# GpSimd's order in an attention loop turned round: normalisation of a unit ahead of the moments of the next one

## The chip, the cores and the metric

The kernel runs on one core of a Trainium2 chip. The metric is the time of one execution on the device in microseconds. Three runs are given by their median. One more execution was recorded by the hardware profiler, and all that is read from a trace comes from it.

## The reference

`x` and `ctx` are (128, 64, 128) in float32: 128 sequences of 64 rows with 128 features. Two layers follow each other.

```
x = x + xattn0(layernorm(x), ctx, ctx)     # layer norms on q and kv, 16 heads of 8, sigmoid gate, layer norm on the output
x = x + ffn0(layernorm(x))                 # silu(w1 x) * (w2 x), two 512x512 with gelu, back to 128
x = x + xattn1(layernorm(x), ctx, ctx)     # 16 heads of 8, no gate, no norm of ctx
x = x + ffn1(layernorm(x))                 # relu(x W1 + b1) W2 + b2
```

`layernorm` takes mean and variance of each row. The attention is a full softmax over the 64 rows of the same sequence.

## The kernel before

`x` lies in SBUF for the whole run as 64 tiles of 128 rows. The kernel is a row of stages: preparation of the weights, attention of layer 0, its feed-forward part, attention of layer 1, its feed-forward part. Each stage is a block in which the five engines have an instruction list of their own, and only semaphores order one engine against another.

`attention(nc, t, layer, front)` is one function for both layers; `gated` is true in layer 0. It works on units of two tiles (256 rows, four sequences), so N = 32 units. On every engine a function `step(j)` is unrolled for j = −5 to N + 3, and one step holds work of several units in different phases. The order within a step is written by hand, and each engine takes its list strictly in order (a later instruction doesn't overtake one that waits).

A unit i goes through these phases:

- VectorE takes the statistics of x, in layer 0 of ctx too (L827), and aggregates them to mean and variance (L842, gives `moments_ready`) in step i − 5.
- GpSimd makes from them minus the mean (L709), the variance with epsilon added (L712, L713 or L715), the power −0.5 of it (L717, `rstd`) and their product (L721, `offset`, gives `offset_ready`), also in step i − 5. The power and the product wait on a chain semaphore for the operation before.
- GpSimd normalises the tiles in step i − 4 (L730, `normed`, gives `normed_ready`): four 128x128 operations in layer 0 (two tiles of x, two of ctx), two in layer 1. `normed` has two slots, so this waits for `in_t_done` of the unit two before.
- TensorE transposes `normed` into the PSUM bank `ps_turn` (L556, gives `in_t_done`) in step i − 3, ScalarE takes it to SBUF (L643, `turned`).
- In step i − 2 TensorE makes the gate (L574, layer 0 only), values (L608), queries and keys (L613, L614); ScalarE takes them; SyncE copies queries and keys into a block layout with DMAs (L904).
- In step i TensorE makes the scores (L513 ahead of all else in the step), VectorE takes the maximum of each row (L765, `top`), TensorE transposes it (L580), and VectorE and ScalarE split it in two parts (L649, L795), which SyncE lays out by DMA (L893).
- In step i + 1 TensorE starts PSUM with the negated maximum (L588), adds the scores again in the other orientation (L513), and ScalarE takes the exponential (L660).
- In step i + 2 TensorE multiplies with the values (L541), ScalarE takes the result (L634, `av`), TensorE turns it (L597), VectorE divides by the sums (L810, L812, `heads_out`).
- In step i + 3: L529, L629 and the output projection (L564), its bias and statistics on VectorE (L784, L834, L848, L853), the power for the output's norm on GpSimd (L737, `y_scale`). In step i + 4 VectorE scales it and adds it to x (L774, `y_gain`, and L802). In layer 1 it is only the sum (L788).
- GpSimd adds the closing bias to the rows of x (L742) in step i.

TensorE's order in a step j, shortened to the lines above: scores of j (L513), L529, L541, L556 of j + 3, L564, L574, L580, L588 and L513 of j − 1, L597, L608, L613, L614. L580 and L588 wait for both halves of L765. The next step's scores wait for the exponentials of ScalarE. SyncE's order: L893 of j, the load of ctx for j + 8 (in layer 0 it waits for `normed_ready` of unit j + 4, whose slot it takes), L904 of j + 2.

Of the kernel before, what the change touches and what calls it, by code (L numbers as in the profile page):

```python
# [11 lines left out]
ALU = mybir.AluOpType  # L12
# [6 lines left out]
P = 128  # L19
# [7 lines left out]
UNROLL = 4  # L27
UNIT_TILES = 2
# [5 lines left out]
def wait(eng, sem, count):  # L34

    if isinstance(count, int) and count <= 0:
        return
    eng.wait_ge(sem, count)


def span(i, width):

    return slice(i * width, (i + 1) * width) if isinstance(i, int) else bass.ds(i * width, width)
# [82 lines left out]
def front_power(nc, t, front, pool, i, s):  # L126

    wait(pool, front.spread_ready, i + 1)
    wait(pool, front.norm_ready, i + 1 - front.slots)
    nc.gpsimd.tensor_tensor(front.rstd[:, s, :], front.spread[:, s, :], t.minus_half[:, 0:CHUNK_TILES],  # L130
                            ALU.pow).then_inc(front.rstd_ready, 1)
# [251 lines left out]
def attention(nc, t, layer, front):  # L383
# [10 lines left out]
    NORMS = 2 if gated else 1  # L394
    SEQS = UNIT_TILES * PER_TILE

    def on(i):
        return 0 <= i < N
# [9 lines left out]
    with ExitStack() as ctx:  # L408
        def sb(name, shape, dt=F32):
            return ctx.enter_context(nc.sbuf_tensor(f"{name}{layer}", shape, dt))  # L410
# [4 lines left out]
        def sem(name):  # L415
            return ctx.enter_context(nc.semaphore(f"{name}{layer}"))
# [4 lines left out]
        rstd = sb("rstd", [P, UNROLL, NORMS, UNIT_TILES])  # L421
        minus_mean = sb("minus_mean", [P, UNROLL, NORMS, UNIT_TILES])
        offset = sb("offset", [P, UNROLL, NORMS, UNIT_TILES])
        normed = sb("normed", [P, 2, NORMS, UNIT_TILES, P])
# [13 lines left out]
        ctx_in = sb("ctx_in", [P, UNROLL, UNIT_TILES, P])  # L438
# [21 lines left out]
        offset_ready = sem("offset_ready")  # L460
        normed_ready = sem("normed_ready")
        in_t_done = sem("in_t_done")
# [39 lines left out]
        with nc.Block() as block:  # L502
# [193 lines left out]
            @block.gpsimd  # L696
            def _(pool):
                for s in range(UNROLL):
                    nc.gpsimd.memset(qk_sets[:, s, :, :, :], 0.0).then_inc(zeros_ready, 1)
                nc.gpsimd.tensor_copy(shift[:, :, :].rearrange("p s n -> p (s n)"),  # L700
                                      t.zero[:, 0:1].to_broadcast([P, 1024])).then_inc(zeros_ready, 1)

                def step(j):
                    i = j + 5
                    if on(i):
                        s = i % UNROLL
                        wait(pool, moments_ready, i + 1)
                        wait(pool, normed_ready, i - 3)
                        nc.gpsimd.tensor_scalar(minus_mean[:, s, :, :], moments[:, s, :, :, 0], -1.0, 0.0, ALU.mult, ALU.add)  # L709
                        if gated:  # L710

                            nc.gpsimd.tensor_scalar(spread[:, s, 0, :], moments[:, s, 0, :, 1], 1.0 + EPS, EPS * EPS, ALU.mult, ALU.add)  # L712
                            nc.gpsimd.tensor_scalar(spread[:, s, 1, :], moments[:, s, 1, :, 1], 1.0, EPS, ALU.mult, ALU.add).then_inc(pool_chain, 1)  # L713
                        else:
                            nc.gpsimd.tensor_scalar(spread[:, s, 0, :], moments[:, s, 0, :, 1], 1.0, EPS, ALU.mult, ALU.add).then_inc(pool_chain, 1)  # L715
                        wait(pool, pool_chain, 2 * i + 1)
                        nc.gpsimd.tensor_tensor(rstd[:, s, :, :], spread[:, s, :, :],  # L717
                                                t.minus_half[:, 0:NORMS * UNIT_TILES].rearrange("p (n k) -> p n k", n=NORMS),
                                                ALU.pow).then_inc(pool_chain, 1)
                        wait(pool, pool_chain, 2 * i + 2)  # L720
                        nc.gpsimd.tensor_tensor(offset[:, s, :, :], minus_mean[:, s, :, :], rstd[:, s, :, :], ALU.mult).then_inc(offset_ready, 1)  # L721
                    i = j + 4
                    if on(i):
                        s = i % UNROLL
                        wait(pool, offset_ready, i + 1)
                        wait(pool, in_t_done, i - 1)
                        for n in range(NORMS):
                            for k in range(UNIT_TILES):
                                src = ctx_in[:, s, k, :] if n else t.x[:, span(i * UNIT_TILES + k, P)]
                                last = nc.gpsimd.tensor_scalar(normed[:, i % 2, n, k, :], src, rstd[:, s, n, k:k + 1],  # L730
                                                               offset[:, s, n, k:k + 1], ALU.mult, ALU.add)
                        last.then_inc(normed_ready, 1)
                    i = j - 3
                    if gated and on(i):
                        wait(pool, y_spread_ready, i + 1)
                        wait(pool, x_done, i - 3)
                        nc.gpsimd.tensor_tensor(y_scale[:, i % UNROLL, :], y_spread[:, i % 2, :], t.minus_half[:, 0:UNIT_TILES],  # L737
                                                ALU.pow).then_inc(y_scale_ready, 1)
                    if on(j):
                        wait(pool, normed_ready, j + 1)  # L740
                        rows = t.x[:, span(j, UNIT)].rearrange("p (k d) -> p k d", d=P)
                        nc.gpsimd.tensor_tensor(rows, rows, closing_row.unsqueeze(1).to_broadcast([P, UNIT_TILES, P]), ALU.add).then_inc(biased, 1)  # L742
                    if j == N:
                        front_power(nc, t, front, pool, 0, 0)

                for j in range(-5, N + 4):
                    step(j)
# [663 lines left out]
```

## Time and profile before

| | |
|---|---|
| median of three runs | 1193.12 us (1189.18 to 1199.44) |
| the profiled execution | 1191.88 us, of which the span from first to last instruction is 1190.0 us |
| mean granted clock of TensorE over the span | 0.938 of full speed |
| TensorE matmuls busy | 1010.8 us (85%) |
| VectorE / ScalarE busy | 711.1 us (60%) / 745.3 us (63%) |
| GpSimd busy | 310.1 us (26%) |
| attention of layer 0, its loop with scores | about 59 to 400 us |
| attention of layer 1 | about 780 to 1070 us |

Times in the trace count from the first instruction. "PE" is TensorE's matmuls and "PEld" its weight loads, DVE is VectorE, ACT ScalarE, POOL GpSimd, SPq SyncE's queue of DMA issues. A number in brackets behind a row is the idle time of that engine just before it and who ended it; "issue" means that nothing in the trace ended it. A granted clock of 1.00 is 2.4 GHz and 0.50 is 1.2 GHz; a window with a value between holds both.

### The profile page before, as it was taken

How to read it: one execution, taken by the hardware profiler on the slowest of the kernel's cores; microseconds unless marked ns; L12 is line 12 of the kernel's file. 1: busy time of each engine (PE TensorE's matmuls, PEld its weight loads, DVE VectorE, ACT ScalarE, POOL GpSimd, SP SyncE). 2: the span in 40 equal slices, each digit the busy share in tenths (PEclk: the TensorE clock that was granted, in tenths of full speed). 3: DMA queues.
4: the chain of work that ended last, by engine and by line, in shares of the span. 5: the costliest groups of instructions: out<-in, count | busy, mean ns of one | idle time of the engine just before them, and what ended most of it. 6: DMA issues, size and time to landing. Idle time of an engine off the chain costs nothing. (4 is left out here: it accounts for less than half of the span.)

```text
span 1190.0 us, 42024 instructions
## 1 busy us (share of the span) xinstructions
PE 1010.8 (85%) x16955; PEld 785.3 (66%) x16955; DVE 711.1 (60%) x1894; ACT 745.3 (63%) x1347; POOL 310.1 (26%) x655
## 2 busy tenths in 40 slices
PE   3378878877888579999999999848899898988998
PEld 2356666666666368788788887636666676666886
DVE  4256566566656666666766766324555555448995
ACT  3145455455545568888888888515556565656896
POOL 5644444344441100000000000053233333301110
PEclk8599898899989789999999999958999999998999
DMA  8311111111101000000000000011111111100111
GB/s 246 86 48 40 46 43 35 46 45 40 44 28 34 4 1 1 0 0 0 0 0 0 0 0 1 1 41 54 55 58 52 59 52 56 44 24 5 41 44 54
DMA packets 53367, 42.43 MB, mean 36 GB/s; under 512 B 16784, under 2 KB 42128, under 8 KB 53200
## 3 DMA queue, kind: packets, MB, share of 16 engines
q1 hardware_dynamic: 50976, 39.61, 10.7%
q8 instruction: 127, 2.08, 0.8%
q0 software_dynamic: 352, 0.27, 0.2%
q10 hardware_dynamic: 1872, 0.14, 0.1%
q14 instruction: 40, 0.33, 0.1%
HBM read 16.93 MB, written 4.19 MB: 18 GB/s over the span
## 5 line engine op out<-in xcount | busy, mean ns | idle before, releaser
L765 DVE TENSOR_REDUCE top<-ps_w 128x16 f32<-128x1024 f32 x128 | 150.8, 1219 | 113.9 <-PE ps_w L513 113.9
L915 PE MATMUL g_ps<-g_h_lo,w_hi 128*128 128x512 f32 x512 | 206.8, 404 | 0.0
L916 PE MATMUL g_ps<-g_h_hi,w_hi 128*128 128x512 f32 x512 | 201.7, 394 | 0.0
L1131 DVE TENSOR_TENSOR g_h_lo<-g_h,g_h_hi 128x512 fp32r<-128x512 f32 x192 | 132.6, 691 | 91.8 <-ACT g_h_hi L1079 87.8
L660 ACT ACTIVATE prob_t<-ps_w 128x1024 f32<-128x1024 f32 x128 | 124.1, 1021 | 86.3 <-PE ps_w L513 83.7
L513 PE MATMUL ps_w<-qk_sets,qk_t 32*64 32x128 f32 x8192 | 161.7, 288 | 3.9 <-ACT prob_t L660 3.5
L513 PEld LDWEIGHTS ps_w<-qk_sets,qk_t 32*64 32x64 f32 x8192 | 129.5, 136 | 42.8 <-issue 41.4
L130 POOL TENSOR_TENSOR front_rstd<-front_spread,minus_half 128x4 f32<-128x4 f32 x32 | 33.4, 1044 | 405.2 <-DVE front_spread L123 405.2
L1079 ACT ACTIVATE g_h_hi<-g_h 128x512 fp32r<-128x512 f32 x192 | 121.4, 632 | 18.7 <-DVE g_h L1141 14.7
L915 PEld LDWEIGHTS g_ps<-g_h_lo,w_hi 128*128 128x128 f32 x512 | 96.9, 189 | 23.1
L916 PEld LDWEIGHTS g_ps<-g_h_hi,w_hi 128*128 128x128 f32 x512 | 96.9, 189 | 20.6
L1071 ACT ACTIVATE g_h<-g_ps,s 128x512 f32<-128x512 f32 x128 | 87.3, 682 | 30.2 <-PE g_ps L916 24.3
L556 PE MATMUL ps_turn<-ident,normed 128*128 128x128 f32 x192 | 38.8, 316 | 78.2 <-POOL normed L730 78.1
L709 POOL TENSOR_SCALAR minus_mean<-moments 128x4 f32<-128x4 f32 (+1 forms) x64 | 12.4, 194 | 313.3 <-DVE moments L842 313.3
L643 ACT ACTIVATE turned<-ps_turn 128x512 f32<-128x512 f32 (+1 forms) x64 | 31.2, 488 | 89.3 <-PE ps_turn L556 89.3
L556 PEld LDWEIGHTS ps_turn<-ident,normed 128*128 128x128 f32 x192 | 22.1, 152 | 88.0 <-POOL normed L730 84.1
L541 PE MATMUL ps_av<-prob_t,v_by_pair 128*32 128x64 f32 x4096 | 72.9, 221 | 8.4 <-issue 8.0
L541 PEld LDWEIGHTS ps_av<-prob_t,v_by_pair 128*32 128x32 f32 x4096 | 61.1, 110 | 20.8 <-issue 19.5
L810 DVE RECIPROCAL rden<-ps_mid 128x32 f32<-128x32 f32 x64 | 22.9, 358 | 86.4 <-PE ps_mid L597 86.4
L634 ACT ACTIVATE av<-ps_av 128x512 f32<-128x512 f32 x64 | 38.2, 597 | 54.1 <-PE ps_av L541 54.1
L1141 DVE SCALAR_TENSOR_TENSOR g_h<-g_ps,s,g_silu 128x512 f32<-128x512 f32 x64 | 46.6, 749 | 35.2 <-ACT g_silu L1101 33.3
L613 PE MATMUL ps_mid<-turned,wa 128*128 128x256 f32 x128 | 48.4, 462 | 15.3 <-DVE heads_out L812 14.9
(178 smaller groups left out, 2089.6 us busy)
## 6 DMA issues: line engine op xcount, KB each, us to landing
qk_sets<-qk_t SPq DMA_DIRECT2D x256, 64.0 KB, 1.9
ctx_in<-in_ctx SPq DMA_DIRECT2D x32, 128.0 KB, 2.2
ctx_in<-in_ctx_t SPq DMA_DIRECT2D x32, 128.0 KB, 2.2
out_x<-x_res SPq DMA_DIRECT2D x16, 256.0 KB, 2.3
raw_mid<-in_L_ffn_h_w SPq DMA_DIRECT2D x2, 1024.0 KB, 10.2
shift<-minus_top_hi SPq DMA_DIRECT2D x128, 8.0 KB
shift<-minus_top_lo SPq DMA_DIRECT2D x128, 8.0 KB
x_res<-in_x SPq DMA_DIRECT2D x2, 512.0 KB, 10.5
```

The costliest lines, as they stand in the source:

```text
L513: done = nc.tensor.matmul(ps_w[h2 * SEQ:(h2 + 1) * SEQ, g * 512 + m * P:g * 512 + (m + 1) * P], qk_t[rows, s, left, at], qk_sets[rows, s, ...
L541: last = nc.tensor.matmul(ps_av[PAIR_COLS * c:PAIR_COLS * (c + 1), (2 * k + half) * P + b * SEQ:(2 * k + half) * P + (b + 1) * SEQ], t.v_b ...
L556: last = nc.tensor.transpose(ps_turn[:, (2 * n + k) * P:(2 * n + k + 1) * P], normed[:, i % 2, n, k, :], t.ident[:, :])
L613: nc.tensor.matmul(ps_mid[:, 0:UNIT], wq, turned[:, i % 2, 0, :], start=True, stop=True)
L660: nc.scalar.activation(prob_t[:, 2 * half:2 * half + 2, :, :, :, :].rearrange("p g k b m q -> p (g k b m q)"), ps_w[:, half * 1024:(half + ...
L765: nc.vector.tensor_reduce(out=top[:, i % 2, half, :], in_=ps_w[:, half * 1024:(half + 1) * 1024].rearrange("p (a q) -> p a q", q=SEQ), op= ...
L915: nc.tensor.matmul(out, w_hi, x_lo, start=first and w_lo is None, stop=False)
L916: return nc.tensor.matmul(out, w_hi, x_hi, start=False, stop=last)
L1071: nc.scalar.activation(h[:, o % 2, :], bank(o), ACT.Gelu, scale=t.s[:, 1 + level, o:o + 1]).then_inc(act_ready[level], 1)
L1079: nc.scalar.activation(h_hi[level][:, o, :], h[:, o % 2, :], ACT.Copy).then_inc(hi_ready[level], 1)
L1131: nc.vector.tensor_tensor(h_lo[level][:, o, :], h[:, o % 2, :], h_hi[level][:, o, :].bitcast(F32), ALU.subtract).then_inc(lo_ready[level], 1)
L1141: nc.vector.scalar_tensor_tensor(out=h[:, o % 2, :], in0=bank(pair(o) + 1), scalar=t.s[:, 1, o:o + 1], in1=silu[:, o % 2, :], op0=ALU.mult ...
```

## The change

In GpSimd's `step(j)` of the attention two blocks change places. Before, the moments of unit j + 5 (L704 to L721) came first and the normalisation of unit j + 4 (L722 to L732) second. Now the normalisation of unit j + 4 comes first. Each block keeps its own waits and instructions, and the rest of the step (`y_scale`, the closing bias) stays behind both. It holds for both layers; no other engine's list changes. At the first units it means that unit 0 is normalised ahead of the moments of unit 1.

```
--- before.py
+++ after.py
@@ -701,6 +701,17 @@
                                       t.zero[:, 0:1].to_broadcast([P, 1024])).then_inc(zeros_ready, 1)
 
                 def step(j):
+                    i = j + 4
+                    if on(i):
+                        s = i % UNROLL
+                        wait(pool, offset_ready, i + 1)
+                        wait(pool, in_t_done, i - 1)
+                        for n in range(NORMS):
+                            for k in range(UNIT_TILES):
+                                src = ctx_in[:, s, k, :] if n else t.x[:, span(i * UNIT_TILES + k, P)]
+                                last = nc.gpsimd.tensor_scalar(normed[:, i % 2, n, k, :], src, rstd[:, s, n, k:k + 1],
+                                                               offset[:, s, n, k:k + 1], ALU.mult, ALU.add)
+                        last.then_inc(normed_ready, 1)
                     i = j + 5
                     if on(i):
                         s = i % UNROLL
@@ -719,17 +730,6 @@
                                                 ALU.pow).then_inc(pool_chain, 1)
                         wait(pool, pool_chain, 2 * i + 2)
                         nc.gpsimd.tensor_tensor(offset[:, s, :, :], minus_mean[:, s, :, :], rstd[:, s, :, :], ALU.mult).then_inc(offset_ready, 1)
-                    i = j + 4
-                    if on(i):
-                        s = i % UNROLL
-                        wait(pool, offset_ready, i + 1)
-                        wait(pool, in_t_done, i - 1)
-                        for n in range(NORMS):
-                            for k in range(UNIT_TILES):
-                                src = ctx_in[:, s, k, :] if n else t.x[:, span(i * UNIT_TILES + k, P)]
-                                last = nc.gpsimd.tensor_scalar(normed[:, i % 2, n, k, :], src, rstd[:, s, n, k:k + 1],
-                                                               offset[:, s, n, k:k + 1], ALU.mult, ALU.add)
-                        last.then_inc(normed_ready, 1)
                     i = j - 3
                     if gated and on(i):
                         wait(pool, y_spread_ready, i + 1)
```

## Rows read from the trace of the kernel before

**Rows 1.** Waits, whole run: who waited for whom, us in total, times, longest.

```profile
...
PE ps_turn L556 <- POOL normed L730: 78.1, 30, 19.4
...
```

**Rows 2.** Waits from 55 to 400 us, layer 0's attention.

```profile
...
PE ps_turn L556 <- POOL normed L730: 41.6, 26, 1.9
...
```

**Rows 3.** Timeline of a layer 0 step: start, length, engine, line, [idle before].

```profile
...
278.76 0.36 DVE L810 RECIPROCAL rden<-ps_mid 128x32 f32<-128x32 f32 x1 [0.89 <-PE ps_mid L597]
...
281.11 0.20 POOL L709 TENSOR_SCALAR minus_mean<-moments 128x4 f32<-128x4 f32 x1 [5.36 <-DVE moments L842]
...
281.94 2.35 DVE L765 TENSOR_REDUCE top<-ps_w 128x16 f32<-128x1024 f32 x2 [0.59 <-PE ps_w L513]
...
284.05 0.88 POOL L730 TENSOR_SCALAR normed<-ctx_in,rstd,offset 128x128 f32<-128x128 f32 x2
...
284.98 0.66 PE L556 MATMUL ps_turn<-ident,normed 128*128 128x128 f32 x4 [1.68 <-POOL normed L730]
...
285.62 1.08 DVE L774 SCALAR_TENSOR_TENSOR y_gain<-y,y_moments,ln_o_g 128x128 f32<-128x128 f32 x2 [1.33 <-POOL y_scale L737]
...
286.79 0.27 PE L580 MATMUL ps_turn<-ident,top 128*32 128x128 f32 x1
...
```

**Rows 4.** Windows between starts of L588: length, each engine's busy time, granted clock.

```profile
...
core 0: us, PE busy (x) PEld busy (x) DVE busy (x) ACT busy (x) POOL busy (x), PEclk, DMA share, GB/s
79.16:353.73 274.57, 221.96 (x5876) 170.70 (x5875) 174.80 (x564) 139.75 (x300) 121.94 (x276) 0.94 0.13 42
99.89:111.65 11.76, 9.73 (x237) 7.48 (x237) 7.09 (x24) 5.59 (x12) 4.87 (x11) 0.85 0.13 39
276.46:286.99 10.53, 8.32 (x237) 6.39 (x237) 7.08 (x24) 5.59 (x12) 4.88 (x11) 1.00 0.15 45
286.99:297.48 10.49, 8.27 (x237) 6.36 (x236) 7.09 (x24) 5.58 (x12) 4.88 (x11) 1.00 0.15 45
353.73:363.50 9.77, 8.45 (x237) 6.44 (x236) 5.73 (x16) 5.55 (x12) 3.06 (x5) 1.00 0.10 32
830.00:1000.00 170.00, 154.46 (x4703) 116.34 (x4705) 89.38 (x201) 100.29 (x204) 59.37 (x147) 1.00 0.18 55
1010.15:1018.29 8.14, 7.52 (x230) 5.69 (x229) 4.39 (x10) 4.94 (x10) 2.85 (x7) 1.00 0.17 52
817.95:1052.47 234.52, 212.46 (x6410) 159.76 (x6410) 121.73 (x268) 137.64 (x278) 75.59 (x182) 1.00 0.17 53
...
```

**Rows 5.** Timeline of a layer 1 step: the late row maximum.

```profile
...
1018.09 0.27 PE L580 MATMUL ps_turn<-ident,top 128*32 128x128 f32 x1 [0.33 <-DVE top L765]
...
```

**Rows 6.** Timeline of the step of layer 0's last unit.

```profile
...
353.02 1.01 POOL L730 TENSOR_SCALAR normed<-x_res,rstd,offset 128x128 f32<-128x128 f32 x2
...
354.02 1.37 POOL L730 TENSOR_SCALAR normed<-ctx_in,rstd,offset 128x128 f32<-128x128 f32 x2
...
354.55 0.59 DVE L802 SCALAR_TENSOR_TENSOR x_res<-y_gain,y_scale,x_res 128x128 f32<-128x128 f32 x2
...
361.24 0.32 PE L541 MATMUL ps_av<-prob_t,v_by_pair 128*32 128x64 f32 x7 [0.78 <-issue]
...
361.49 0.66 PE L556 MATMUL ps_turn<-ident,normed 128*128 128x128 f32 x4
...
```

**Rows 7.** Timeline of the first step of layer 0's loop.

```profile
...
67.38 2.36 DVE L765 TENSOR_REDUCE top<-ps_w 128x16 f32<-128x1024 f32 x2 [2.23 <-PE ps_w L513]
...
69.09 0.66 PE L556 MATMUL ps_turn<-ident,normed 128*128 128x128 f32 x4 [1.75 <-POOL normed L730]
...
70.90 0.27 PE L580 MATMUL ps_turn<-ident,top 128*32 128x128 f32 x1
...
```

**Rows 8.** Timeline of layer 0's start on GpSimd.

```profile
...
39.76 0.19 POOL L709 TENSOR_SCALAR minus_mean<-moments 128x4 f32<-128x4 f32 x1
...
41.81 0.89 POOL L730 TENSOR_SCALAR normed<-x_res,rstd,offset 128x128 f32<-128x128 f32 x2
...
```

**Rows 9.** Timeline of layer 1's start on GpSimd.

```profile
...
782.68 0.19 POOL L709 TENSOR_SCALAR minus_mean<-moments 128x2 f32<-128x2 f32 x1
...
784.16 0.88 POOL L730 TENSOR_SCALAR normed<-x_res,rstd,offset 128x128 f32<-128x128 f32 x2
...
```

## The prediction

> **What bounds the kernel now.** I went from the whole to one step: first the list of waits, then one step of layer 0 in order of time, then windows from step to step, and last the steps that lack one piece of it.
>
> The list of waits names the place. TensorE stood idle ahead of the transposes L556 for 78.1 us in 30 places until GpSimd's normed was there, once for 19.4 us at a layer's start [rows 1]. Within layer 0's loop it is 41.6 us in 26 places [rows 2]. In layer 1 only the start has it.
>
> One step of layer 0 in order of time shows a ring [rows 3]. GpSimd stands idle for 5.36 us until VectorE has aggregated the moments of unit j + 5 (L842). It starts on them (L709) at 281.11, and only when it is through with them does it normalise unit j + 4, whose rstd and offset it has held since the step before; it ends at 284.05 + 0.88 = 284.93. L556 begins at 284.98, after 1.68 us of nothing, and ScalarE's L643, the gate's matmuls, L580 and L588 follow it. In the next turn the second pass over the scores, L597 and VectorE's L810, L812 and L827 lie ahead of the next moments. The ring goes once through VectorE, GpSimd, TensorE and ScalarE, and takes 10.53 us from L588 to L588, with the granted clock at 1.00; such steps take 10.49 to 10.53 [rows 4], and I go on with 10.50.
>
> Layer 1 has nearly the same program. Its step takes 8.14 us (the window 1010.15 to 1018.29) and its L556 has no wait; what is late there is the row maximum, by 0.33 us ahead of L580 [rows 4, 5]. Its GpSimd has two statistics and two normalisations less in a step and is through before L556 is reached. So what the diff turns round bounds layer 0's loop and not layer 1's.
>
> **The change part by part.** No instruction is added or removed, and GpSimd issues no DMA in either block. Its five instructions of moments (in layer 1 four) go behind the four of the normalisation (in layer 1 two). The wait on moments_ready now has the normalisation ahead of it; the wait on in_t_done now has the moments, y_scale and L742 queued behind it.
>
> *Steady steps of layer 0.* In step j the normalisation of unit j + 4 needs the offset of GpSimd's step j − 1 and the in_t_done of unit j + 2, which TensorE gave in its step j − 1, before that step's L588. So it starts as soon as GpSimd is done with the L742 of step j − 1, and TensorE wants it only in step j + 1: most of a step lies between. The in_t_done wait should cost nothing; if it did, the moments would be late by as much, and they too have most of a step. The wait ahead of L556 goes altogether, and L556 follows L541. What is late next? The row maximum L765 ends at 281.94 + 2.35 = 284.29; L580 would come at 286.79 − 1.68 = 285.11 [rows 3], so it keeps 0.8 us. y_scale stands behind 2 × 0.88 us less on GpSimd, so y_gain (L774) no longer waits its 1.33 us for it [rows 3] but starts when L765 is done. Next in line is TensorE's own order with L643 in it: a step of 10.50 − 1.68 = 8.82 us.
>
> The trace of before has this step already, once. Layer 0's last unit is normalised in a GpSimd step that has no moments: at 353.02, and its L556 at 361.49 waits for nothing [rows 6]. This step took 9.77 us from L588 to L588 [rows 4], of which 0.78 us is a gap within L541 [rows 6]: 8.99 us without it, and somewhat less as the weight loads' gap there is longer. So the bounds are 8.82 and 8.99 a step, 0 to 4 us in all. I take the sum of the waits: 41.6, less the first with 1.75 [rows 7], is 39.9 us in 25 steps.
>
> *The first step of the loop.* L556 waits 1.75 us there, but L580 behind it needs L765, which ends at 67.38 + 2.36 = 69.74, where L580 came at 70.90 [rows 7]. With some 0.1 us from one to the other, 1.0 us is gained.
>
> *Starts of the layers.* Unit 0's normalisation stands behind unit 1's moments. In layer 0 those take from 39.76 to 41.81 = 2.05 us [rows 8], in layer 1 from 782.68 to 784.16 = 1.48 us [rows 9], and TensorE waits for it both times. Units 1 and 2 keep the lead, since GpSimd works there without a pause. Together 3.5 us; the loads of ctx behind it could eat all of it at worst, so 0 to 3.5, and I take 3.5 because the load queue itself is released by this normalisation.
>
> *TensorE's clock.* The window from 79.16 to 353.73 has 25 steps in 274.57 us [rows 4]. With the clock always at 1.00 they would be 25 × 10.50 = 262.5. The other 12.1 us lie in ten longer steps, of which one is shown: 11.76 us at a granted clock of 0.85, so partly at 1.2 GHz [rows 4]. Ahead of each fall TensorE had the pause at L556. In layer 1, where TensorE is busy 154.46 of 170 us (91%), the clock stays at 1.00; in layer 0's steps at 1.00 it is 8.32 of 10.53 (79%), and with the wait gone 8.3 of 8.8 (94%) [rows 4]. The bounds are 0 and 12.1 us; I take 12.1, as layer 1 is the nearer row. (The Trainium skill, "TensorE: Matmul & The Clock Gate", section "What's actually happening", has the throttled clock as the default, which activity releases. The rows agree in direction.)
>
> *What comes up from under the wait.* Gaps within L541 that end on no other engine ("issue") are hidden wherever L556 waits for normed anyway. In layer 1 nothing hides them: 28 steps from 817.95 to 1052.47 take 234.52 us against 28 × 8.14 = 227.9 [rows 4], so 6.6 us, 0.24 a step. In 25 steps of layer 0 that is 5.9 us. Part of that is in the 39.9 us already: 25 full waits of 1.68 would be 42.0, and the missing 2.1 us are steps in which such a gap has taken the place of some of the wait. What remains is 3.8 us of cost; bounds 0 and 5.9.
>
> *The rest.* Layer 1's steps: 0, as normed isn't late there, GpSimd's two blocks together are shorter than its idle time, and L765 sets L580. SyncE's load of ctx waits for normed, with the copies to qk_sets queued behind it; both are released sooner, which I count 0, as scores of a unit come two steps after its copies. The feed-forward stages and the preparation don't run this code: 0.
>
> Sum: −39.9 − 1.0 − 3.5 − 12.1 + 3.8 = −52.7 us. The profiled execution took 1191.88 us (its span 1190.0 and 1.9 around it), so 1139.2. The median of the runs is 1193.12, 1.2 more: 1140 us, 4.5% less than before.
>
> **Where VectorE could lose.** Two y_gain operations take 1.08 us beside GpSimd's L742, where two L802 of the same shape take 0.59 [rows 3, 6]. In the new order the normalisation follows L742 at once and lies beside y_gain, L784, L795 and L802. So it did for the last unit: there GpSimd's two pairs took 1.01 and 1.37 us instead of 0.88 each, and VectorE's L802 kept its 0.59 [rows 6]. By the Trainium skill, "SBUF — State Buffer", section "SBUF: two separate sides", a VectorE operation with two SBUF inputs and a GpSimd operation can't share their ports: the one that starts first holds them for its whole length. By that rule VectorE could stand still again and again; the rows show it for y_gain alone.
>
> **The rivals.**
> 1. The wait goes and the clock falls as often as now. For it: smaller pauses at L613, L574 and L541 stay. Against it: layer 1. 1140 + 12.1 = 1152 us.
> 2. VectorE is held up beside the normalisation. Before L810 it has 0.89 us of idle time [rows 3]; four pieces of 0.44 us would make it late by 0.9, half of that 0.4 us in each of 25 steps, so 10 us: 1150. Against it: rows 6.
> 3. Slower than before: at the same place GpSimd's pieces also stretch L812 and the statistics, so that L613, and the next scores behind it, come over 1.68 us late in every step; that is the point from which it costs more than the wait did. At 2.4 us a step and the clock as now it is 25 × 0.7 = 18 us less the 3.5 at the starts: 1208. Against it: GpSimd has 1.8 us of this work in a step, and 0.89 of idle time stands ahead of L810.
> 4. The change doesn't do what it says: another of L556's waits (top_split, out_t_ready, gate_exp_ready, turned_taken) is as late as normed. Only the starts gain: 1190. Against it: the last unit's L556 [rows 6].
>
> **How the numbers follow.** Forecast 0.62, rival 1 0.18, rival 2 0.10, rival 4 0.04, rival 3 0.03; 0.03 is left for more than the forecast (no gap exposed, and a clock that rises sooner in the first steps). The predicted time is the forecast's. The range goes down to 1132 for that and up to 1156, which takes in rivals 1 and 2 with the starts or the 8.99 us step added. A measurement of this kernel can tell about 1% from no change. Faster by over 1%: 0.93 (all but rivals 3 and 4); within 1%: 0.04; slower: 0.03.
>
> **What would show it.** Right: in layer 0 no wait of L556 for normed, L588 to L588 at 8.8 us, the clock at 1.00 from 80 us to the loop's end, y_gain right behind L765, a gap within L541 every few steps that now lengthens its step; layer 1's step still 8.14 us; both first L556 sooner by 2.0 and 1.5 us after GpSimd's first L709. Wrong: over 0.3 us of wait at L613 for heads_out (rival 2 or 3), longer steps at 0.85 (rival 1), L556 waiting for ScalarE or VectorE (rival 4). A new wait of SyncE's copies on which the scores depend would be something I haven't foreseen.

## The result, and the profile after

The changed kernel takes **1130.66 us**, the median of 4 runs (1129.36 to 1136.2); the kernel before took 1191.51 beside it (4 runs, 1189.18 to 1199.44). The ratio is 0.9487, with a 95% interval of 0.9431 to 0.9543: 5.1% faster. Forecast were 1140 us and a range of 1132 to 1156. The direction and the size are near it, but the time lies 1.3 us below the range's lower end. The profiled execution took 1129.89 us (span 1128.0) where that of before took 1191.88 (1190.0): 62.0 us less, where the sum of the prediction gave 52.7. Where these 9.3 us come from is worked out behind the experiments.

In the changed kernel the normalisation is line L712 (L730 before), minus_mean L720 (L709), rstd L728 and offset L732. All other lines keep their numbers.

First the list of waits, whole run, as in [rows 1]:

```profile
...
POOL minus_mean L720 <- DVE moments L842: 237.1, 55, 8.0
...
PE ps_turn L556 <- POOL normed L712: 33.6, 4, 17.4
...
PE ps_mid L613 <- DVE heads_out L812: 16.4, 56, 0.3
...
```

TensorE waited for normed 30 times before, 78.1 us; now 4 times, 33.6 us, of which 17.4 and 11.6 us are the fills of the two layers. From 55 to 350 us, where 41.6 us in 26 places stood [rows 2], no such row is left. L613 waits 0.29 us in a step for heads_out. The forecast named more than 0.3 us there as the sign that VectorE is held up; it isn't.

Next one steady step of layer 0 in order of time, from L588 to L588, which answers to [rows 3]:

```profile
...
209.44 0.51 PE L588 MATMUL ps_w<-shift,halves 32*128 32x512 f32 x4
...
209.75 1.43 POOL L712 TENSOR_SCALAR normed<-ctx_in,rstd,offset 128x128 f32<-128x128 f32 x2
...
210.26 0.59 DVE L802 SCALAR_TENSOR_TENSOR x_res<-y_gain,y_scale,x_res 128x128 f32<-128x128 f32 x2
...
211.12 1.94 ACT L660 ACTIVATE prob_t<-ps_w 128x1024 f32<-128x1024 f32 x2 [1.17 <-PE ps_w L513]
...
212.58 0.70 PE L613 MATMUL ps_mid<-turned,wa 128*128 128x256 f32 x2 [0.29 <-DVE heads_out L812]
...
214.05 0.20 POOL L720 TENSOR_SCALAR minus_mean<-moments 128x4 f32<-128x4 f32 x1 [2.87 <-DVE moments L842]
...
214.88 2.35 DVE L765 TENSOR_REDUCE top<-ps_w 128x16 f32<-128x1024 f32 x2 [0.59 <-PE ps_w L513]
...
216.17 0.66 PE L556 MATMUL ps_turn<-ident,normed 128*128 128x128 f32 x4
...
216.78 0.72 POOL L742 TENSOR_TENSOR x_res<-x_res,ln_o_b 128x256 f32<-128x256 f32 x1
...
217.15 0.77 DVE L774 SCALAR_TENSOR_TENSOR y_gain<-y,y_moments,ln_o_g 128x128 f32<-128x128 f32 x2
217.49 1.02 POOL L712 TENSOR_SCALAR normed<-x_res,rstd,offset 128x128 f32<-128x128 f32 x2
217.52 0.61 PE L574 MATMUL ps_turn<-gate_col,turned 128*128 128x1 f32 x4 [0.24 <-ACT turned L643]
...
217.98 0.27 PE L580 MATMUL ps_turn<-ident,top 128*32 128x128 f32 x1
218.18 0.51 PE L588 MATMUL ps_w<-shift,halves 32*128 32x512 f32 x4
...
```

The step takes 8.74 us where it took 10.5. The normalisation starts behind L742, runs across the boundary of the step and ends at 209.75 + 1.43 = 211.18; L556, which reads it, comes at 216.17 without a wait. That is 5.0 us of lead. GpSimd still stands idle ahead of the moments, 2.87 us in place of 5.36, which costs nothing now. y_gain (L774) starts as L765 ends. The waits that remain on TensorE in a step are 0.29 at L613 and 0.24 at L574.

Then windows between starts of L588, with the columns of [rows 4]. First the kernel after: layer 0's start (from GpSimd's first moments to the first L588), its 25 steps, the rest of the layer, what lies between the layers' loops (the feed-forward stage and the start of layer 1), layer 1's loop, the end, and one single step.

```profile
...
38.65:68.10 29.45, 17.84 (x226) 13.24 (x226) 10.71 (x45) 9.16 (x24) 21.85 (x55) 0.68 0.15 49
76.03:297.78 221.75, 205.86 (x5878) 159.15 (x5877) 165.24 (x564) 138.96 (x300) 134.86 (x272) 1.00 0.16 51
297.78:336.69 38.91, 33.51 (x1045) 25.48 (x1044) 25.30 (x72) 21.85 (x44) 8.69 (x13) 1.00 0.10 30
336.69:749.68 412.99, 369.59 (x1890) 292.93 (x1889) 251.22 (x565) 314.85 (x488) 40.83 (x62) 0.95 0.01 4
749.68:1004.66 254.98, 229.49 (x6977) 172.88 (x6977) 129.85 (x284) 150.03 (x298) 77.65 (x187) 0.99 0.17 51
1004.66:1128.00 123.34, 112.85 (x665) 90.88 (x664) 99.12 (x311) 96.17 (x166) 16.43 (x16) 0.96 0.12 35
209.44:218.18 8.74, 8.21 (x236) 6.35 (x235) 6.68 (x24) 5.55 (x12) 5.57 (x12) 1.00 0.20 61
...
```

The same stretches of the kernel before, as far as [rows 4] lacks them:

```profile
...
37.68:71.10 33.42, 19.71 (x226) 14.69 (x227) 10.71 (x45) 9.14 (x24) 19.93 (x51) 0.62 0.13 40
...
353.73:392.75 39.02, 33.51 (x1045) 25.48 (x1044) 25.29 (x72) 21.81 (x44) 8.60 (x13) 1.00 0.09 28
392.75:809.19 416.44, 374.26 (x1890) 295.65 (x1889) 251.28 (x565) 314.38 (x488) 39.77 (x60) 0.93 0.01 4
809.19:1065.51 256.32, 230.08 (x6977) 173.02 (x6976) 129.97 (x284) 149.75 (x298) 78.43 (x189) 0.99 0.16 51
1065.51:1190.00 124.49, 113.64 (x665) 91.57 (x664) 99.13 (x311) 95.96 (x166) 16.42 (x16) 0.97 0.12 34
...
```

Of the 62.0 us, 52.8 are in the 25 steps of layer 0: 274.57 before, 221.75 now. The granted clock there was 0.94 and is 1.00, and TensorE's busy time for the same instructions fell from 221.96 to 205.86 us. Up to the first L588 it is 3.0 us (71.10 to 68.10) and in the step behind it 0.1. Between the layers it is 3.45, in layer 1's loop 1.34, at the end 1.15 and in the rest of layer 0 0.1.

The starts on GpSimd, which answer to [rows 8] and [rows 9], with what TensorE does in layer 1 soon after:

```profile
...
38.65 0.20 POOL L720 TENSOR_SCALAR minus_mean<-moments 128x4 f32<-128x4 f32 x1 [3.00 <-DVE moments L842]
40.88 0.89 POOL L712 TENSOR_SCALAR normed<-x_res,rstd,offset 128x128 f32<-128x128 f32 x2
...
723.75 0.19 POOL L720 TENSOR_SCALAR minus_mean<-moments 128x2 f32<-128x2 f32 x1
725.38 0.89 POOL L712 TENSOR_SCALAR normed<-x_res,rstd,offset 128x128 f32<-128x128 f32 x2
...
737.76 1.21 PE L513 MATMUL ps_w<-qk_sets,qk_t 32*64 32x128 f32 x64 [1.73 <-DMA qk_sets<-qk_t]
...
```

Unit 0's normalisation now follows its own moments. In layer 0 L588 comes 29.45 us behind the first moments instead of 33.42, in layer 1 25.93 (723.75 to 749.68) instead of 27.99 (781.20 to 809.19). In layer 1 the first scores then wait 1.73 us for SyncE's copies, where they waited 0.35 before; in the second profile of this kernel (further down) they wait 0.35 too.

### The profile page after: what moved, and what is told of

It is laid out like the page before. It is cut to its first block and busy times, and to the rows that moved or that the text cites. A ratio compares the mean times of both kernels' runs of the same rounds, so it can differ in the third digit from the quotient of the medians.

```text
span 1128.0 us, 42024 instructions
## 1 busy us (share of the span) xinstructions
PE 988.0 (88%) x16955; PEld 770.5 (68%) x16955; DVE 701.7 (62%) x1894; ACT 745.8 (66%) x1347; POOL 325.5 (29%) x655
## 5 line engine op out<-in xcount | busy, mean ns | idle before, releaser
L765 DVE TENSOR_REDUCE top<-ps_w 128x16 f32<-128x1024 f32 x128 | 150.8, 1219 | 110.6 <-PE ps_w L513 110.6
L660 ACT ACTIVATE prob_t<-ps_w 128x1024 f32<-128x1024 f32 x128 | 124.1, 1022 | 80.6 <-PE ps_w L513 77.9
L513 PE MATMUL ps_w<-qk_sets,qk_t 32*64 32x128 f32 x8192 | 155.8, 280 | 6.1 <-ACT prob_t L660 3.5
L513 PEld LDWEIGHTS ps_w<-qk_sets,qk_t 32*64 32x64 f32 x8192 | 124.7, 131 | 43.4 <-issue 40.0
L1079 ACT ACTIVATE g_h_hi<-g_h 128x512 fp32r<-128x512 f32 x192 | 121.6, 633 | 18.7 <-DVE g_h L1141 14.6
L720 POOL TENSOR_SCALAR minus_mean<-moments 128x4 f32<-128x4 f32 (+1 forms) x64 | 12.5, 196 | 237.1 <-DVE moments L842 237.1
L541 PE MATMUL ps_av<-prob_t,v_by_pair 128*32 128x64 f32 x4096 | 72.6, 221 | 7.2 <-issue 6.8
L541 PEld LDWEIGHTS ps_av<-prob_t,v_by_pair 128*32 128x32 f32 x4096 | 61.0, 110 | 19.5 <-issue 18.1
L556 PE MATMUL ps_turn<-ident,normed 128*128 128x128 f32 x192 | 37.1, 305 | 34.2 <-POOL normed L712 33.6
L613 PE MATMUL ps_mid<-turned,wa 128*128 128x256 f32 x128 | 47.2, 452 | 16.4 <-DVE heads_out L812 16.4
L712 POOL TENSOR_SCALAR normed<-x_res,rstd,offset 128x128 f32<-128x128 f32 x128 | 60.1, 476 | 1.1
L643 ACT ACTIVATE turned<-ps_turn 128x512 f32<-128x512 f32 (+1 forms) x64 | 31.2, 488 | 43.8 <-PE ps_turn L556 43.8
```

The costliest lines, as they stand in the source:

```text
L513: done = nc.tensor.matmul(ps_w[h2 * SEQ:(h2 + 1) * SEQ, g * 512 + m * P:g * 512 + (m + 1) * P], qk_t[rows, s, left, at], qk_sets[rows, s, ...
L541: last = nc.tensor.matmul(ps_av[PAIR_COLS * c:PAIR_COLS * (c + 1), (2 * k + half) * P + b * SEQ:(2 * k + half) * P + (b + 1) * SEQ], t.v_b ...
L613: nc.tensor.matmul(ps_mid[:, 0:UNIT], wq, turned[:, i % 2, 0, :], start=True, stop=True)
L660: nc.scalar.activation(prob_t[:, 2 * half:2 * half + 2, :, :, :, :].rearrange("p g k b m q -> p (g k b m q)"), ps_w[:, half * 1024:(half + ...
L765: nc.vector.tensor_reduce(out=top[:, i % 2, half, :], in_=ps_w[:, half * 1024:(half + 1) * 1024].rearrange("p (a q) -> p a q", q=SEQ), op= ...
L1079: nc.scalar.activation(h_hi[level][:, o, :], h[:, o % 2, :], ACT.Copy).then_inc(hi_ready[level], 1)
```

## The experiments

The theory: the whole gain of the loop is the pause ahead of L556 plus the clock that the pause let fall; behind it stand TensorE's own order and the gaps in it that end on nothing in the trace. The rivals are those of the prediction. "Before" in each comparison is the kernel before, timed beside it.

**Which part of the order matters.** Three kernels take the new order in a part of the steps only, and the old one elsewhere:

```diff
 def step(j):
...
+    if gated:        # layer 0 only;  second kernel: not gated;  third: j < 0
+        take_normed()
+        take_moments()
+    else:
+        take_moments()
+        take_normed()
```

Layer 0 alone:

> New order in layer 0's attention only, layer 1 as before. Theory A (the gain is layer 0's ring, its start and the clock there; layer 1 gives its start alone): 1130.7 plus the 1.5 us of layer 1's start, 1132 us; layer 0's steps 8.74 us with the clock at 1.00. Rival B (the order also helps layer 1's loop, where the changed kernel's 31 steps were 1.3 us shorter in all): 1134 or more.

Measured: 1133.3 us (4 runs, 1129.89 to 1137.95) against 1191.19, ratio 0.9504 (0.9447 to 0.9561). Its steps take 8.74 us, and five of 25 are longer, by gaps like these in TensorE's timeline:

```profile
...
145.37 0.65 PE L541 MATMUL ps_av<-prob_t,v_by_pair 128*32 128x64 f32 x30 [1.12 <-issue]
...
166.10 0.66 PE L556 MATMUL ps_turn<-ident,normed 128*128 128x128 f32 x4 [1.16 <-issue]
...
```

The step with the first of them takes 10.15 us. The 25 steps are 225.35 us long, 6.7 more than 25 × 8.745. So layer 0 carries the gain.

Layer 1 alone:

> New order in layer 1's attention only, layer 0 as before. Theory A: before less 1.5 us, 1190 us, layer 1's step still 8.14 us, layer 0's wait of 1.68 us and its falls of the clock still there. Rival B: 1188 or less, with fewer or shorter gaps in layer 1's loop.

Measured: 1190.24 us, ratio 0.9993 (0.9965 to 1.002). One of its 10 runs took 3108.96 us, for which no profile shows a cause; the median doesn't feel it. Layer 1's loop takes 255.58 us and its start 25.87. Nothing that the time can tell.

The steps with j below 0 alone, in both layers:

> New order only in the steps ahead of the first scores (j < 0), in both layers; the order of before from j = 0 on. Theory A: the starts give 2.0 and 1.5 us and the loop nothing, 1188 us. The first step of the loop has its wait at L556 again. Rival: loads or ScalarE eat the lead at the starts, 1191 us.

Measured: 1189.06 us (10 runs), ratio 0.9974 (0.9947 to 1.0001): 2 to 3 us, at the edge of what can be told. In the profile layer 0's start takes 32.22 us (33.42 before) and layer 1's 25.88 (27.99).

**Is it the pause that lets the clock fall?** The old order, with 11 transposes of the identity put ahead of the wait for normed in the steps of layer 0. They write to ps_turn, which L556 then overwrites; they add work that nobody uses.

```diff
-    wait(pe, normed_ready, i + 1)
...
     wait(pe, top_split, j)
     if gated:
         wait(pe, gate_exp_ready, j + 2)
+        if j >= 0:
+            for k in range(11):
+                nc.tensor.transpose(ps_turn[:, (k % 4) * P:(k % 4 + 1) * P], t.ident[:, :], t.ident[:, :])
+    wait(pe, normed_ready, i + 1)
```

> The order of before. In layer 0's loop TensorE makes 11 transposes of the identity into the bank that L556 overwrites, ahead of its wait for normed, so that most of the pause is filled with work that nobody needs. If the falls of the clock come from the pause: no falls between 80 and 350 us, each step still about 10.5 us, 1191.5 less 12 = 1179 us. If the falls have another cause: 1191 us and windows at 0.85 still there. If the eleven take over 1.76 us, steps are longer than 10.5 by the rest.

Measured: 1180.01 us (8 runs, 1178.8 to 1186.06), ratio 0.9922 (0.989 to 0.9954). The window over the 25 steps, and two rows of TensorE in time order (L555 are the added transposes, L559 is the old L556):

```profile
...
80.59:347.50 266.91, 241.34 (x6152) 189.72 (x6151) 174.66 (x564) 139.70 (x300) 122.52 (x276) 1.00 0.14 42
...
```

```profile
...
109.91 0.66 PE L559 MATMUL ps_turn<-ident,normed 128*128 128x128 f32 x4 [0.35 <-POOL normed L733]
...
119.77 1.42 PE L555 MATMUL ps_turn<-ident 128*128 128x128 f32 x11
...
```

The ring through normed is as long as before: steps of 10.51 us, still a wait of 0.35. But the clock is 1.00 in every step where it was 0.94, and the kernel is faster by 11 us with 1.42 us more work in each step. The longer steps at the lower clock are gone, 12.1 us in the window by [rows 4]; in their place 25 steps take 266.91 us against 25 × 10.51 = 262.75. These 4.2 us lie in eight steps in a row, each with a gap of 0.6 to 1.0 us that ends on nothing. 12.1 − 4.2 is about the 7.7 us by which the window shrank (274.57 to 266.91). The other 4.3 us between the spans (1190.0 to 1178.0) are a balance: the rest of layer 0's attention is 1.7 us longer (the loop's first step took 10.09 us at a clock of 0.83, where it had 8.06 at 1.00), and the stages that the edit doesn't touch are 6.0 us shorter, which differ from one execution to the next by as much (below).

**The ring made longer.** Moments, y_scale and L742 first, the normalisation last:

```diff
 def step(j):
-    [normalise unit j + 4]
     [moments of unit j + 5]
     [y_scale of unit j - 3, L742 of unit j]
+    [normalise unit j + 4]
```

> GpSimd's step is moments, y_scale, closing bias, normalisation. If the ring (moments of the next unit, GpSimd, L556, L588, next moments) is what bound the kernel before, then the 0.70 and 0.72 us of y_scale and bias now lie in it as well: layer 0's steps 10.50 + 1.42 = 11.9 us, 1191 + 25 x 1.42 = 1227 us, a few more if the clock falls more often. Rival (the order matters only through the contention with VectorE, or through the wait on moments as such): 1191 or less.

Measured: 1269.63 us (2 runs), ratio 1.0658 (1.0532 to 1.0785). The window over 25 steps, and one wait:

```profile
...
80.59:433.29 352.70, 278.31 (x5876) 214.81 (x5875) 165.45 (x564) 141.57 (x300) 124.68 (x274) 0.75 0.10 32
...
```

```profile
...
117.02 1.12 PE L556 MATMUL ps_turn<-ident,normed 128*128 128x128 f32 x4 [3.16 <-POOL normed L740]
...
```

The pause is 3.16 us here (2.8 in the mean of the 25 steps), as the two instructions put ahead of the normalisation (0.70 + 0.72) make it. With it a step would be 8.745 + 3.16 = 11.9 us at full clock. The first of the 25 takes 10.91 us, the others 14.0 to 14.6, at a mean granted clock of 0.75. The L556 of this row takes 1.12 us where it takes 0.66 at 1.00. The ring was understood, the price of the clock wasn't: with a pause of 3.2 us it falls in 24 of 25 steps, which costs each another 2.1 to 2.7 us.

**Is GpSimd's work off the path?** Every normalisation is made twice, first into a spare tensor, in the new order and in the old one:

```diff
+        if i >= 2:
+            wait(pool, normed_ready, i)
         wait(pool, in_t_done, i - 1)
+        for n in range(NORMS):
+            for k in range(UNIT_TILES):
+                nc.gpsimd.tensor_scalar(spare[:, n, k, :], src, rstd[:, s, n, k:k + 1], offset[:, s, n, k:k + 1], ALU.mult, ALU.add)
         for n in range(NORMS):
             for k in range(UNIT_TILES):
                 last = nc.gpsimd.tensor_scalar(normed[:, i % 2, n, k, :], src, rstd[:, s, n, k:k + 1],
...
```

In the new order:

> The order of the change, and each normalisation made twice (once into a spare tensor), four more GpSimd operations a step in layer 0, two in layer 1. If GpSimd's block lies off the path with 2.87 us of idle time behind it: steps of layer 0 stay at 8.74 us; only the starts of the layers grow, by some 3.5 and 1.8 us: 1136 us. If VectorE is held up by GpSimd's work beside it (the rival of the prediction): y_gain, L802 or L812 longer, a wait at L613 over 0.29 us, steps over 8.9 us, 1140 to 1170 us.

Measured: 1137.81 us (4 runs, 1135.88 to 1139.66), ratio 0.9546 (0.946 to 0.9633). One step in time order (the added line is L715, the moments L728):

```profile
...
122.74 1.44 POOL L715 TENSOR_SCALAR spare<-ctx_in,rstd,offset 128x128 f32<-128x128 f32 x2
...
125.58 0.70 PE L614 MATMUL ps_mid<-turned,wa 128*128 128x256 f32 x2 [0.29 <-DVE heads_out L820]
...
127.06 0.20 POOL L728 TENSOR_SCALAR minus_mean<-moments 128x4 f32<-128x4 f32 x1 [1.17 <-DVE moments L850]
...
```

GpSimd's idle time shrinks from 2.87 to 1.17 us; the step stays at 8.74 and the wait behind VectorE at 0.29. In the profile, 19 of the 25 steps are 8.73 to 8.75 us long, and the other six hold 6.3 us more. Four of them have a gap of 0.4 to 1.1 us that ends on nothing. The other two each follow a step with a gap of 1.05 or 1.06 us and take 9.93 and 10.02 us at granted clocks of 0.83 and 0.85, 2.5 us in all; that is why the mean clock is 0.98.

In the old order:

> The order of before, each normalisation made twice. The 1.76 us lie in the ring: steps of layer 0 of 12.3 us, 25 x 1.76 = 44 us, starts 5 us, so 1240 us; more if the clock falls more often in the longer pause. Layer 1 gets 0.88 us, of which its slack at L556 and L580 takes most.

Measured: 1289.81 us (2 runs), ratio 1.0828 (1.0701 to 1.0955).

```profile
...
87.65:450.09 362.44, 280.33 (x5876) 217.72 (x5876) 175.90 (x564) 141.48 (x300) 166.25 (x377) 0.74 0.10 31
...
```

The same 1.7 us of GpSimd work costs 98 us in the old order and 7 in the new one (1137.81 − 1130.66). The first of the 25 steps takes 12.96 us, the others 14.3 to 14.8: the ring is longer by the doubled part, and the clock falls in each of them.

**What bounds the new step?** By the prediction it is TensorE's own order with ScalarE's L643 in it. This kernel has the new order, moves the gate's matmuls (L574) behind the values (L608), so that they don't stand between L643 and L580, and ScalarE's exponential of the gate with them:

```diff
+    if gated:                              # ahead of L529
+        wait(pe, gate_exp_ready, upto(j + 2))
...
-    if gated and on(j + 2):
-        [gate matmuls of unit j + 2]       # ahead of L580
...
     last.then_inc(v_done, 1)
+    if gated:
+        wait(pe, top_split, j + 1)
+        [gate matmuls of unit i]           # behind L608
     wait(pe, heads_ready, j - 1)
...
-            wait(dve, gate_exp_ready, upto(j + 3))
+            wait(dve, gate_exp_ready, upto(j + 2))
```

> The order of the change, and in layer 0 the gate's matmuls (L574) moved from ahead of L580 to behind the values (L608), into the pause of 0.29 us at L613; ScalarE's exponential of the gate goes behind its copies of the values. If TensorE's own order is the bound now: L580 and L588 0.46 us sooner after the scores, L613 0.2 us later after L588, steps of 8.5 us, 1130.7 less 7 = 1124 us. If another ring holds at 8.74 us (ScalarE's copies, the row maximum): 1131 us or more.

Measured: 1125.3 us (4 runs, 1124.81 to 1127.96), ratio 0.9452 (0.9367 to 0.9538). TensorE in one step:

```profile
...
203.03 0.68 PE L615 MATMUL ps_mid<-turned,wa 128*128 128x256 f32 x2
...
207.95 0.28 PE L576 MATMUL ps_turn<-ident,top 128*32 128x128 f32 x1 [0.24 <-ACT turned L645]
208.17 0.51 PE L584 MATMUL ps_w<-shift,halves 32*128 32x512 f32 x4
```

A step takes 8.38 us, where 8.5 was expected. The gate's matmuls now lie where TensorE waited 0.29 us for heads_out, and that wait is gone. So TensorE's chain, with what it waits for within the step (0.24 us for ScalarE's L643, now ahead of L580), is indeed what bounds it, and the step is shorter by 0.36 us. ScalarE's exponential of the gate moved too, but it wasn't on the path: in the changed kernel ScalarE stood idle for 1.17 us behind it, ahead of L660.

**The change once more**, beside the next kernel on another chip:

> The changed kernel once more, unaltered, for its spread and a second trace. If the miss of the prediction is a property of the kernel: median within 1130 to 1132 us, 25 steps of layer 0's loop in 222 us. If part of it is the draw of one execution (gaps that end on nothing, TensorE's clock in the feed-forward stages): the 25 steps between 221 and 226 us, the median 1131 to 1135 us.

Measured: 1129.87 us (6 runs, 1128.31 to 1132.31) against 1189.46 (11 runs), ratio 0.9504 (0.9474 to 0.9534). The start and the 25 steps of its profile:

```profile
...
38.82:66.71 27.89, 16.05 (x226) 12.21 (x227) 10.71 (x45) 9.14 (x24) 20.61 (x53) 0.75 0.15 47
74.68:294.78 220.10, 205.74 (x5876) 159.07 (x5875) 164.83 (x564) 138.64 (x300) 135.23 (x272) 1.00 0.17 51
...
```

Both the median and the 25 steps lie a little below what was expected either way. 23 of the 25 steps take 8.73 to 8.75 us and two are longer, by 0.67 and 0.9: 1.5 us in all. The start takes 27.89 us at a clock of 0.75, where the profile above has 29.45 at 0.68, and 33.42 at 0.62 before.

**A version that is faster than both.** The kernel with the gate's matmuls moved, and in layer 1 the transposes L597 of unit j − 2 ahead of L580, where TensorE waited 0.33 us for the row maximum [rows 5]:

```diff
+    i = j - 2
+    if not gated and on(i):
+        [transposes of av, the old L597]   # ahead of the transposes of top
...
-    if on(i):
+    if gated and on(i):
         [transposes of av, the old L597]
```

> e8's kernel, and in layer 1 TensorE's transposes L597 moved from behind L588 and the second pass to ahead of L580, into the pause in which it waits for the row maximum. If layer 1's step is the ring row maximum, L588, L597, heads_out, L613, scores: L588 0.1 us later after the scores, the next scores 0.45 us sooner after L588 (then held by the exponentials), steps of 7.8 us for 8.14, 28 steps: 1125.3 less 9 = 1116 us. If the exponentials or TensorE's work bound layer 1 already: 1125 us or more.

Measured: 1118.71 us (6 runs, 1116.86 to 1121.48), ratio 0.9404 (0.9374 to 0.9434), against 0.9504 for the change alone beside it. Most of layer 1's steps take 7.77 to 7.9 us in place of 8.14; its loop takes 250.01, 5.2 less than with the gate's matmuls alone, where 9 were expected. What is late next, in TensorE's timeline of layer 1:

```profile
...
844.02 0.66 PE L576 MATMUL ps_mid<-ident,av 128*128 128x128 f32 x4
844.67 0.28 PE L585 MATMUL ps_turn<-ident,top 128*32 128x128 f32 x1
...
848.74 1.20 PE L513 MATMUL ps_w<-qk_sets,qk_t 32*64 32x128 f32 x64 [0.54 <-ACT prob_t L666]
...
```

The wait ahead of L580 (here L585) is gone, and 0.4 to 0.6 us of wait for ScalarE's exponentials (L666) stand ahead of the second pass instead. It is 1.0% below the change and 6.0% below the kernel before.

## Why the prediction was right in kind and short in size

**The bound was the ring through normed in layer 0.** Right. With the new order in layer 0 alone the ratio is 0.9504, in layer 1 alone 0.9993. Work added to the normalisation costs 98 us in the old order and 7 in the new.

**The wait goes altogether, and TensorE's own order is next.** Right in kind. Rival 4 (another wait as late) is out, since L556 waits for nothing. That the chain on TensorE is the next bound is shown by the gate's matmuls: moved out of it, they give 0.36 us a step.

**The step of 8.82 us.** This is the first term that was mis-sized. It measured 8.745. The pause was read off the matmul row of L556, 1.68 us [rows 3]; the weight load of the same instruction, which goes ahead of the matmuls on its own row, had waited longer in the kernel before:

```profile
...
284.98 0.42 PEld L556 LDWEIGHTS ps_turn<-ident,normed 128*128 128x128 f32 x4 [1.84 <-POOL normed L730]
...
```

With nothing to wait for, that load hides beside L541, and L556 starts sooner than 1.68 us ahead of its old place: 2.53 us behind the start of the next unit's scores (213.64 to 216.17) where it was 4.29. That is 1.76 us, and 10.505 − 1.76 = 8.745. In 25 steps the difference is 1.9 us. The bound on the other side, 8.99 from the last unit's step, was a step with a gap and wasn't approached.

**The gaps that come up.** The second mis-sized term. Forecast were 5.9 us in the 25 steps, 3.8 of them net, after layer 1's rate. Measured over 25 × 8.745 = 218.6: 3.1 us in the changed kernel, 1.5 when it was run again, 6.7 with the new order in layer 0 alone, and 6.3 with the doubled normalisation (2.5 of them falls of the clock). So the rate of layer 1 lay within what occurs, and this kernel's executions had few. Why one execution has more of them than another no run has settled. Nor is it shown that as many lay under the wait before: the trace of before has two of them in its 25 steps (0.73 and 0.89 us, both within L541), which took the place of 1.6 us of the wait, and the filled pause has eight. A gap within the wait itself the trace couldn't tell from the wait.

**The clock.** Right. Rival 1 (falls as often as now) is out: 1.00 over the 25 steps in the changed kernel both times, with the new order in layer 0 alone and with the gate moved. With the old ring and TensorE kept busy in the pause it is 1.00 as well, and with the new order it still fell twice behind a gap of 1.05 us (doubled normalisation). So it is the pause and not the order of GpSimd that let it fall. The term of 12.1 us is one draw: over the same 25 steps in the old order the profiles of the kernels with the change in layer 1 alone and in the first units alone took 273.06 and 279.16 us, which is 10.6 and 16.7 over 262.5.

**VectorE beside the normalisation.** Rival 2 is out, and so is rival 3. In the step above L802 keeps its 0.59 us, y_gain takes 0.77 for its two in place of 1.08, and the wait at L613 is 0.29. It is mostly GpSimd that is stretched: its pairs of normalisations take 1.02 and 1.43 us where they took 0.88 each, as [rows 6] had it, and GpSimd has 2.87 us to spare. By the rule of the Trainium skill that the prediction weighed ("SBUF — State Buffer", section "SBUF: two separate sides"), the engine that comes second waits. The trace agrees for L742: it starts 0.06 us ahead of the first y_gain, which then takes 0.81 us in the kernel before, against 0.34 for the second. It doesn't agree for the normalisation: within the pair of 1.43 us the second operation starts at 210.18, ahead of the two L802 at 210.26, and yet it is the one that takes longer, 1.00 us for 0.45. Between 80 and 290 us of the changed kernel this is so each time: wherever an L802 lies beside a normalisation (40 times), GpSimd started first and the L802 kept its length.

**Starts and first step.** Forecast were 3.05 us up to layer 0's first L588 and 1.48 in layer 1. Counted from GpSimd's first moments it is 3.97 us in layer 0 and 5.5 in the second profile of the change; in the profile of the result the first moments came 0.97 us later than before, so 3.0 us are left of it in the sum. That it comes so near the forecast is partly luck. With the old order this start took 33.42, 34.05 and 32.80 us (before, layer 1 alone, and the filled pause, which has 22 of its transposes in it), with the new one 27.89 and 29.45 in the changed kernel and 30.62, 31.17, 32.22 and 32.54 in four others (layer 0 alone, gate moved, first units, last version). The granted clock in it was 0.60 to 0.75 with the old order and 0.55 to 0.75 with the new. So a gain is there, but that the clock rises sooner with the new order, to which the prediction gave 0.03 together with "no gap exposed", isn't shown. The step behind it depends on the clock as well: 7.93 to 8.06 us at 1.00, 9.6 to 11.4 at 0.60 to 0.74, in kernels of either order.

In layer 1 the gain is 2.06 us against 1.48. Of its starts, the old order took 27.99, 26.31 and 27.28 us (before, layer 0 alone, filled pause), the new one 25.87 to 25.94 in five kernels and 26.78 in the second profile of the change. At the same granted clock it is 27.99 against 26.78 (0.54), and 26.31 against 25.87 and 25.88 (0.63): 0.4 to 1.2 us. The prediction counted SyncE's copies at 0, and the wait of 1.73 us for them didn't come from the new order alone: in the second profile the first scores begin 13.98 us behind the first moments after 0.35 us of wait, in the first 14.01 after 1.73, and before it was 15.20.

**What the sum left out.** The 9.3 us between 62.0 and 52.7 are then: 1.9 (step), 2.8 (gaps), 0.1 (start and first steps of layer 0), 0.1 (rest of layer 0), 0.6 (layer 1's start), and 3.9 us in the feed-forward stage, layer 1's loop and the end, where the diff changes nothing that is late (each rounded). For these the sum had no term. Kernels with and without the new order took 413.0 to 416.4 us between the layers' loops, 253.0 to 258.1 in layer 1's loop and 122.9 to 124.5 at the end. The profile of before stood at the top of the first and the last, the profile of the change at the bottom of the first. So the profiled execution that the sum started from was a long one in those places, and the median of three to which 1.2 us were added was too: 1193.12, where 4, 6, 11 and 23 runs gave 1191.51, 1191.74, 1189.46 and 1191.19. By medians taken side by side the gain is 60.9 us (1191.51 to 1130.66) and 59.6 (1189.46 to 1129.87), so 7 to 8 us over the sum's 52.7, of which the step and the gaps make 4.7. What failed is thus the sizing, and with it the range: the step's bounds (8.82 and 8.99) had nothing below 8.82, the gaps were taken at layer 1's full rate, and a lower end 8 us under the forecast had no room for both and for the spread of the untouched stages.

## What to carry to other kernels

In a loop with a ring over several engines, put first on each engine what another engine waits for and whose inputs are already there, and leave for later what itself waits; here that was 5% for no change of work. A pause of TensorE is worth more than its length where the granted clock falls behind it: price it from a step at each level, and if it can't be closed, filling it with idle transposes gives back part (here 11 us of 60). Read a pause off the weight load's row as well as off the matmul's, and before a range is set see how far stages that the change doesn't touch differ between executions.

## What the runs showed of the hardware

- **Clock and pause.** With 1.76 us of pause in a step of 10.5 us, 10 of 25 steps were longer, up to 12.05 us, at a mean clock of 0.94 over the 25 (0.91 and 0.94 in two other profiles of that order). With 3.2 us (normalisation last) and with the doubled one in the old order 24 of 25 were, at mean clocks of 0.75 and 0.74, and each cost 2 us or more beyond its pause. With the pause filled it was 1.00 throughout. With the new order a gap of 1.05 us was followed by a fall twice (doubled normalisation), gaps of 1.1 to 1.2 us in layer 0 alone by none.
- **Gaps that end on nothing.** They are up to 1.2 us long, ahead of or within L541, L556 or L564, and what makes them no run shows. In the changed kernel they stand at 83.84, 94.01, 163.70, 234.34 and 305.19 us, most of them some eight steps apart; in the filled pause they came in eight steps in a row.
- **GpSimd beside VectorE.** A pair of GpSimd's 128x128 normalisations took 0.88 us beside L765, 1.02 beside y_gain and 1.43 beside L802 and L795. L802 kept its 0.59 us for two in it though GpSimd had started first. GpSimd's L742, where it started first, made the first y_gain 0.81 us long instead of 0.34.
